# A matrix-memory attention head in which TensorE's high/low products stand together, and so do its plain ones

## The reference

```python
grads = jax.vmap(jax.grad(chunk_loss), ...)(mem_ws, keys, lr, values)   # of a two-layer memory, per chunk
momentum = _assoc_scan(mom_gate, -grads)          # over the chunks
updates  = _assoc_scan(1.0 - decay, momentum)
w0, w1 = mem_w0 + updates[0], mem_w1 + updates[1]
x    = einsum('bhncd,bhnde->bhnce', q, w0)
vals = einsum('bhncd,bhnde->bhnce', silu(x), w1)
vals = _rmsnorm(vals) * (mh_gamma + 1.0) * gate
out  = vals.transpose(...) @ w_combine
```

## Time and profile before

| what | before |
|---|---|
| median of three runs | 1265.42 us |
| the profiled execution's span | 1264.6 us |
| TensorE, busy | 1127.4 us (89%) |
| TensorE weight loads | 922.8 us (73%) |
| VectorE | 741.5 us (59%) |
| ScalarE | 682.3 us (54%) |
| GpSimd | 589.8 us (47%) |

### The profile page before, as it was taken

One profiled execution on the slowest core, in us unless ns is written; L12 is line 12 of the kernel. 1 busy time (PEld: TensorE's weight loads), 2 busy tenths in 40 slices (PEclk: granted clock), 3 DMA queues, 4 the chain that ended last, 5 costly groups with the idle time before them and its releaser, 6 DMA issues. The chain is left out here.

```text
span 1264.6 us, 21008 instructions
## 1 busy us (share of the span) xinstructions
PE 1127.4 (89%) x6645; PEld 922.8 (73%) x6646; DVE 741.5 (59%) x1913; ACT 682.3 (54%) x1355; POOL 589.8 (47%) x568
## 2 busy tenths in 40 slices
PE   4689746999999999999999999999999999968980
PEld 3356534888888888888888888888888888858980
DVE  4488856656655555555556555565555566545546
ACT  4567523555555555555555555555555555534541
POOL 2166752777544444444444444444444444433553
PEclk9688857999999999999999999999999999998995
DMA  9033204000000000000000000000000000004434
GB/s 197 28 91 93 83 25 144 20 22 18 17 1 1 2 7 0 0 7 0 0 0 7 0 0 0 7 0 0 7 0 0 0 7 1 2 8 128 142 96 133
DMA packets 65604, 40.92 MB, mean 32 GB/s; under 512 B 4300, under 2 KB 61974, under 8 KB 65431
## 3 DMA queue, kind: packets, MB, share of 16 engines
q1 hardware_dynamic: 57783, 31.30, 9.5%
q0 software_dynamic: 2304, 4.74, 1.2%
q10 hardware_dynamic: 5472, 4.33, 1.0%
HBM read 22.49 MB, written 15.77 MB: 30 GB/s over the span
## 5 line engine op out<-in xcount | busy, mean ns | idle before, releaser
L1022 DVE TENSOR_TENSOR p_sb<-bank,cf 128x512 f32<-128x512 f32 (+3 forms) x512 | 218.8, 480 | 1.0 <-PE bank L877 1.0
L1104 POOL TENSOR_TENSOR qa_low<-qa,qa_high 128x450 fp32r<-128x450 f32 x64 | 94.4, 1475 | 119.1 <-ACT qa_high L986 119.1
L1112 POOL TENSOR_TENSOR rs<-ms,neg_half 128x4 f32<-128x4 f32 x64 | 84.7, 1324 | 128.6 <-DVE ms L1032 128.6
L1031 DVE TENSOR_SCALAR ms<-bank 128x3 f32<-128x3 f32 x64 | 10.3, 161 | 213.4 <-PE bank L959 213.4
L900 PE MATMUL bank<-p_sb,du_t 128*128 128x450 f32 (+3 forms) x512 | 132.0, 401 | 0.0
L1128 POOL TENSOR_TENSOR sq_rest<-sq,sq_high 128x450 f32<-128x450 f32 x64 | 67.1, 1048 | 135.0 <-ACT sq_high L999 135.0
L900 PE MATMUL bank<-p_sb,err_t 128*128 128x450 f32 (+3 forms) x512 | 128.8, 394 | 0.4 <-DVE p_sb L1022 0.4
L900 PEld LDWEIGHTS bank<-p_sb,du_t 128*128 128x128 f32 x512 | 82.0, 190 | 44.7 <-issue 32.7
L900 PEld LDWEIGHTS bank<-p_sb,err_t 128*128 128x128 f32 x512 | 87.1, 190 | 37.0 <-issue 23.6
L1050 DVE SCALAR_TENSOR_TENSOR acc<-bank,rg,acc 128x128 f32<-128x128 f32 x224 | 62.7, 344 | 71.6 <-POOL rg L1116 71.6
L1132 POOL TENSOR_TENSOR sq_low<-sq_rest,sq_mid 128x450 bf16<-128x450 f32 x64 | 66.4, 1038 | 75.4 <-ACT sq_mid L1007 75.3
(11 more groups left out here) (295 smaller groups left out, 3204.4 us busy)
## 6 DMA issues: line engine op xcount, KB each, us to landing
x<-in_L_attn_inputs SPq DMA_DIRECT2D x16, 256.0 KB, 3.0
rows<-sorted_rows SPq DMA_DIRECT2D x40, 64.5 KB
sorted_rows<-xl_all SPq DMA_DIRECT2D x1, 2064.0 KB, 18.6
x_rows<-x SPq DMA_DIRECT2D x8, 256.0 KB, 2.4
xn_rows<-xn SPq DMA_DIRECT2D x8, 256.0 KB, 2.4
xl_all<-xl SPq DMA_DIRECT2D x8, 256.0 KB, 3.3
ew<-in_L_ffn_w SPq DMA_DIRECT2D x8, 256.0 KB, 4.3
xn_all<-xn_rows SPq DMA_DIRECT2D x8, 256.0 KB
```

Source lines behind the costliest of these rows:

```text
L1022: last = nc.vector.tensor_tensor(dst, src, w, ALU.mult)
L1104: nc.gpsimd.tensor_tensor(parts[1][:], whole[:], parts[0][:], ALU.subtract).then_inc(done, 1)
L1112: nc.gpsimd.tensor_tensor(rs[:], ms[:], m.neg_half[:, 0:T], ALU.pow).then_inc(g_rs, 1)
```

## The change

TensorE does the same matmuls in another order. The plain tiles 2 and 3 of both score blocks are taken out of the score block and put behind the split products that followed: on the side of `s` behind `VB`, `w_qk` and `EB` products, and on the side of `f` behind `w_x` and the transposes of `du`. The `VB` product moves ahead of `w_qk`. The plain tiles stand in the order 2, 3 and share bank 6; the counts are given by tiles 0, 1 and 3. On ScalarE the copy `err_t` moves from behind `sq_high` to before it.

```diff
--- before.py
+++ after.py
@@ -36,10 +36,11 @@
 V_ROWS = V_EB1 + E * FB
 
 
-SC_BANK = [4, 5, 6, 5]
-SC_COL = [0, 0, 0, 384]
+SC_BANK = [4, 5, 6, 6]
+SC_COL = [0, 0, 0, 256]
 P_COL = [0, 512, 1024, 896]
-SC_ORDER = [0, 1, 3, 2]
+SC_ORDER = [0, 1, 2, 3]
+SC_SPLIT = [0, 1]
 SC_BANKS = 3
 P_COLS = sum(S - P * i for i in range(T))
 
@@ -882,26 +883,27 @@
                     y = [part[:, bass.ds(at[0], 1), first:first + width].rearrange("p a n -> p (a n)") for part in m.y_all]
                     return product(out[:, 0:width], [part[:, at[1], :] for part in w], y, stop=stop)
 
-                def scores(left_2, right_2, left, right, done, tiles=SC_ORDER):
+                def scores(left_2, right_2, left, right, done, tiles):
 
                     for i in tiles:
                         out = m.bank[SC_BANK[i]][:, SC_COL[i]:SC_COL[i] + QW - P * i]
-                        if i < 2:
+                        if i in SC_SPLIT:
                             last = product(out, [part[:, i * P:i * P + P] for part in left_2], [part[:, P * i:] for part in right_2])
                         else:
-                            last = pe.matmul(out, left[:, (i - 2) * P:(i - 1) * P], right[:, P * i:], start=True, stop=True)
-                        if i != 1:
+                            last = pe.matmul(out, left[:, (i - len(SC_SPLIT)) * P:(i - len(SC_SPLIT) + 1) * P], right[:, P * i:], start=True, stop=True)
+                        if i != 2:
                             last.then_inc(done, 1)
 
                 def apply(out, rows, made, n):
                     for i in SC_ORDER:
                         if i != 3:
-                            pe.wait_ge(made, SC_BANKS * n + {0: 1, 1: 2, 2: 3}[i])
+                            pe.wait_ge(made, SC_BANKS * n + i + 1)
                         last = pe.matmul(out[:, P * i:QW], rows[:, i, :], p_sb[:, P_COL[i]:P_COL[i] + QW - P * i],
                                          start=False, stop=True, skip_group_check=True)
                     return last
 
                 def step(f, s, z):
+                    plain = SC_ORDER[len(SC_SPLIT):]
                     if f is not None:
                         h, n = f[1], n_of(f)
                         pe.wait_ge(v_du, n)
@@ -912,7 +914,9 @@
                         k = n_of(s)
                         pe.wait_ge(v_xl, k + 1)
                         pe.wait_ge(v_p0, SC_BANKS * (k + 1))
-                        scores(s_2[s[1] % 2], xs_2, s_sb[s[1] % 2][:, 2 * P:], xs, p_s1)
+                        scores(s_2[s[1] % 2], xs_2, None, None, p_s1, SC_SPLIT)
+                        pe.wait_ge(v_ms, k)
+                        product(VB[:, 0:QW], [w[:] for w in w1], [part[:] for part in xs_2])
                     if f is not None:
                         if isinstance(n, int) and n < 2:
                             pass
@@ -922,9 +926,8 @@
                         pe.wait_ge(g_sl, n + 1)
                         product(EB[:], [w[:] for w in w1], [part[:] for part in s_2[h % 2]], start=False).then_inc(p_e, 1)
                     if s is not None:
-                        pe.wait_ge(v_ms, k)
+                        scores(None, None, s_sb[s[1] % 2][:, len(SC_SPLIT) * P:], xs, p_s1, plain)
                         pe.wait_ge(a_et, k + 1)
-                        product(VB[:, 0:QW], [w[:] for w in w1], [part[:] for part in xs_2])
                         apply(VB, err_t, v_p1, k).then_inc(p_v, 1)
                     if f is not None:
                         pe.wait_ge(a_err, n + 1)
@@ -939,14 +942,14 @@
                             pe.wait_ge(v_y, 3 * (f[0] + 1))
                         pe.wait_ge(g_ql, n + 1)
                         pe.wait_ge(v_p1, SC_BANKS * n)
-                        scores(yk, qa_2, yb, qa, p_s0, SC_ORDER[:-1])
+                        scores(yk, qa_2, None, None, p_s0, SC_SPLIT)
+                        pe.wait_ge(a_et, n + 1)
+                        project(XB, m.w_x, f, SHIFT)
                         pe.wait_ge(v_du, n + 1)
                         for t in range(T):
                             last = pe.transpose(EB[:, t * P:t * P + P], du[:, t * P:t * P + P], m.ident[:])
                         last.then_inc(p_dt, 1)
-                        scores(yk, qa_2, yb, qa, p_s0, SC_ORDER[-1:])
-                        pe.wait_ge(a_et, n + 1)
-                        project(XB, m.w_x, f, SHIFT)
+                        scores(None, None, yb, qa, p_s0, plain)
                         pe.wait_ge(a_dt, n + 1)
                         apply(XB, du_t, v_p0, n).then_inc(p_x, 1)
                     if s is not None:
@@ -995,11 +998,13 @@
                         nc.scalar.copy(vals[:], VB[:, 0:QW]).then_inc(a_v, 1)
                         act.wait_ge(a_v, k + 1)
                         nc.scalar.activation(sq[:], vals[:], ACT.Square).then_inc(a_sq, 1)
+                    if f is not None:
+                        act.wait_ge(p_et, n + 1)
+                        nc.scalar.copy(err_t[:].rearrange("p t d -> p (t d)"), XB[:]).then_inc(a_et, 1)
+                    if s is not None:
                         act.wait_ge(a_sq, k + 1)
                         nc.scalar.copy(sq_3[0][:], sq[:]).then_inc(a_hi, 1)
                     if f is not None:
-                        act.wait_ge(p_et, n + 1)
-                        nc.scalar.copy(err_t[:].rearrange("p t d -> p (t d)"), XB[:]).then_inc(a_et, 1)
                         act.wait_ge(p_dt, n + 1)
                         nc.scalar.copy(du_t[:].rearrange("p t d -> p (t d)"), EB[:]).then_inc(a_dt, 1)
                     if s is not None:
@@ -1018,9 +1023,9 @@
                         dst = p_sb[:, P_COL[i]:P_COL[i] + C * ch].rearrange("p (c n) -> p c n", n=C)
                         w = cf[:, h, i * NC + 2 * i:i * NC + NC].unsqueeze(2).broadcast_to([P, ch, C])
                         if i != 3:
-                            dve.wait_ge(made, SC_BANKS * n + {0: 1, 1: 2, 2: 3}[i])
+                            dve.wait_ge(made, SC_BANKS * n + i + 1)
                         last = nc.vector.tensor_tensor(dst, src, w, ALU.mult)
-                        if i != 1:
+                        if i != 2:
                             last.then_inc(done, 1)
 
                 def step(f, s, z):
```

## The result

The changed kernel took 1320.86 us (median of 4 runs, 1318.09 to 1322.5); the kernel before, on the same chip in between, 1265.74 (4 runs, 1263.39 to 1267.59). The ratio is 1.043, with a 95% interval of 1.041 to 1.045. It is slower, by 55 us. Two executions behind the experiments, one of the kernel before and one of the version with both waits away, took 3.9 and 3.7 ms; no figure here counts them.

What follows compares the result with a forecast made beforehand. TensorE was taken as the bound, busy 908.17 of the attention stage's 922 us. 63 x 0.27 = 17.0, 64 x 0.44 = 28.2 and 7 x 0.73 = 5.1, together 50.3 us, on 1265.42 gave 1315.7 us, range 1289 to 1340.

Steps and rivals of the forecast that it cites:

- Both waits: In each steady head TensorE would newly wait for `err_low` (0.27 us) and for `du_t` before `apply` (0.44 us).
- Is anything lost at changes of type?: TensorE's switches between split and plain matmuls, four fewer a head: taken at 0 us each, 0.14 at most.
- The rival that fewer changes pay: Four fewer type changes a head gain time, faster kernel above 0.20 us each; chance 0.05 visible price, 0.04 over 0.20.
- First move: Store side's plain tiles behind `w_qk` and `EB`: late tiles delay `q_sb` and `err_low`, TensorE's `err_high` product 0.27 us later.
- The rival that the collision stays: On the store side `qa_low` still meets the second `q_sb` or `err_low`: 63 x 0.45 us more, 1344; chance 0.08.
- Second move: Retrieve side's `w_x` ahead of the `du` transposes: they start 0.44 us later in the chain, and `apply` waits for `du_t`.
- The rival that only the second wait shows: Only the retrieve side's 0.44 us a head counts, `err_low` getting back all 1.23 us: 1293.6 us; chance 0.10.
- the one in which nothing changes: The waits in attention turn out covered and the time stays at 1265.4 us; chance 0.03.
- Together 0.71 a head: All behind `apply` in a steady head moves 0.71 us later, from 0.27 on the store and 0.44 on the retrieve side.
- Edits at nothing: Earlier `err_t` copy, later `sq_high`, order 2, 3 and shared bank cost nothing; at most 0.58 us if `sq_high` lost cover.
- Head 0 of a batch: Four extra VectorE copies leave no idle time before `err_low`: store shift 1.00 us instead of 0.27, in 7 heads.

Runs made afterwards that it cites:

- the version with both waits away: Changed kernel with `q_sb` early (in first heads of a batch `yk`, `yb` instead) and the `du` transposes ahead of `w_x`: 1253.3 us.
- The store side alone: Changed kernel with the retrieve side's matmul order put back, so only the `s` side's plain tiles and `VB` moved: 1291.6 us.
- The retrieve side alone: Changed kernel with the store side's matmul order put back, so only `w_x` and the `f` side's plain tiles moved: 1294.13 us.
- the kernel with both moves undone: Changed kernel with all matmuls back in place; shared bank, order 2, 3, counts and earlier `err_t` copy stay: 1264.36 us.
- the version with more changes of type: Kernel before, with tile 3 of the retrieve side between split tiles 0 and 1, two more changes a head: 1267.58 us.
- the ungrouped kernel with the two VectorE edits: Kernel before, TensorE's order untouched, with `q_sb` between tiles 1 and 3 and the first head's copies behind `err_low`: 1248.08 us.

## Why the prediction was right

The forecast was 1315.7 us in a range of 1289 to 1340, and the time is 1320.86. The sum had 50.3 us; the profiled spans differ by 56.2. Both waits came where they were forecast and at their forecast size in steady heads. What is missing from the sum lies in the eight first heads of the batches.

- **Is anything lost at changes of type?** I took 0, with 0.14 as the far bound. Two more a head cost 2.45 us in 64 heads, 0.02 a change (0.03 at most by the interval), and most of it is likely a short tile's. The rival that fewer changes pay, which decides at 0.20 us, is out by a factor of seven at least.
- **First move, 0.27 a head.** In the head above, tile 2 starts at 5.52 us (forecast 723.98 - 718.43 = 5.55), `q_sb` at 6.06 (6.08), `err_low` ends at 8.06 (8.08), the product is at 8.12 (8.14): 0.25 later than before. The store side alone had 0.25 in its steady head. That `err_low` would fall to 0.68 was the step on which 0.45 us hung: it is 684 ns at the shortest and at the median. The rival that the collision stays is out. The margin against it was forecast at 0.07 us and turned out as nothing: `qa_low` was done at 758.03, as the second `q_sb` started. That it didn't collide was in part luck; by the argument of the forecast, which no run tested, a meeting so late would have cost little.
- **Second move, 0.44 a head.** The retrieve side alone had 14.86 against 14.41, 0.45. The transposes came 0.69 later and `du_t` 0.69, for 0.71; `apply` came 0.66 later. The rival that only the second wait shows (1293.6) is out by the two single moves, and so is the one in which nothing changes.
- **Together 0.71 a head:** over the 55 heads that are not the first of a batch the periods grew by 0.70 in the mean.
- **Edits at nothing:** 1264.36 against 1265.13, within what can be told from no change.
- **Head 0 of a batch, 1.00 + 0.44 = 1.44:** here the step failed. The seven grew by 2.05 in the mean, 4.2 us more in all. The retrieve part was right (0.45 in the single move), the store part was 1.61 for 1.00. I moved the four copies later by 1.23 us and did not ask what they would then stand beside. They landed on `qa_low`, which now starts 0.09 us after tile 2 does, and `yk_high` waited it out: 0.57 of the missing 0.60. I had cited the rule for the instructions that I knew to collide, and not run the moved ones past it. "SBUF — State Buffer" of the Trainium skill, section "SBUF: two separate sides", counts a VectorE copy of fp32 from SBUF to SBUF among those that shut GpSimd out and are shut out by it; these rows agree, with 844 ns at the median for 278 before.
- **The very first head** grew by 3.03 us (12.86 to 15.89) and not by 0.44. Most of this is the clock's and not the order's. TensorE has stood idle for 17.1 us when that head starts, in both kernels, and the granted clock of the stretch is 0.55 after: nearly all of it at the lower of the two levels, 1.2 and 2.4 GHz. The same stretch of the kernel before:

```profile
199.60:214.00 14.40, 12.53 (x50) 9.41 (x50) 5.60 (x13) 7.28 (x12) 2.41 (x2) 0.81 0.95 287
```

  and of the kernel with both moves undone, whose first head was 15.47 at a median of 1264.36:

```profile
199.60:214.00 14.40, 13.18 (x41) 9.81 (x41) 4.83 (x9) 5.30 (x10) 2.42 (x2) 0.58 1.02 301
```

  From 216 us on after has 1.00 too. When the clock comes back differs between executions of like work: with both moves undone this head took 2.61 us more than in the kernel before. Heads with a like clock over their own length can be compared. At 0.58 the kernel with both moves undone took 15.47, and at 0.59 the changed one 15.89, 0.42 more. At 0.75 it is 13.95 in the version with more changes of type and 14.40 in that with the retrieve side alone, 0.45 more. But at 0.80 it is 12.86 in the kernel before, and at 0.79 13.68 in the changed kernel with `q_sb` early, 0.82 more. So 0.4 to 0.8 of the 3.03 us are the order's, for a forecast of 0.44, and the rest is the clock's. With one profile of each kernel this stays an estimate, and why the clock came back later is open.

By these parts the 56.2 us are 55 x 0.70 = 38.5 for the heads that are not the first of a batch, 14.3 for the seven first heads, 3.0 for the very first, and 0.4 outside of them and in the last.

## What to carry to other kernels

Before instructions of the bound engine are regrouped, follow the count that each releases: here matmuls that cost nothing to move held the tiles of an engine that works in order, and with them the one operand that everything waited for. Whatever slips later on that engine has to be checked against what the other engines do at its new time, down to the copies of one head in eight. And when such a regrouping has lost, look for the instruction behind the wait that doesn't need it: with `q_sb` ahead of the late tiles, `err_low` ahead of the copies and `du`'s transposes back ahead of `w_x` the kernel went from 1320.9 to 1243.6 us with its plain tiles still grouped, and ended 4.5 below the ungrouped kernel with the two VectorE edits.

## What the runs showed of the hardware

- A change between fp32r and fp32 matmuls cost TensorE 0.03 us at most, in a place where nothing hides it (two more a head: 2.45 us in 64 heads, with an interval up to 3.7).
- The matmul behind a plain tile of 66 columns takes some 0.05 to 0.08 us longer to the next start, whatever its type: 0.23 us instead of 0.15 for a split one, 0.218 instead of 0.164 for a plain one. With tile 2 ahead of tile 3, `apply` follows the pair at 756.58 - 756.08 = 0.50 us. For the old order, where the tile of 194 columns stands behind that of 66, the same pair inside `apply` takes 0.55 in the kernel before. Why the matmul is late was not tested.
- Which VectorE instructions wait for GpSimd's subtractions hangs on their operands: `err_low` (two SBUF inputs) 684 or 1098 ns, fp32 copies from SBUF to SBUF 280 or 844 (`yk_high`) and 281 or 624 (`cf`), but tiles 2 and 3, whose input is a bank, took 0.62 us beside `qa_low` in the changed kernel, which is the 0.416 and 0.279 of the earlier trace rows less their overlap.
